# The first unit of a fused adaLN, linear attention and mixture-of-experts kernel: a new order for its zero products, norms, roundings and weight halves

## What the reference computes

```python
# x: (2, 2048, 256), 16 heads of 16, 8 experts of width 128, top 2
mod = (silu(c) @ wmod).reshape(2, 6, 1, 256)
sa, ca, ga, sb, cb, gb = (mod[:, k] for k in range(6))
ga, gb = (sign(g) * maximum(abs(g), 0.25) for g in (ga, gb))
h = layernorm(x) * (1 + ca) + sa
Q, K, V = (h @ W.T + b for W, b in ((Wq, bq), (Wk, bk), (Wv, bv)))
Q, K = elu(Q) + 1, elu(K) + 1
KV = einsum('bshd,bshe->bhde', K, V)
Z = 1 / (einsum('bshd,bhd->bsh', Q, K.sum(axis=1)) + 1e-6)
x = x + ga * (einsum('bshd,bhde,bsh->bshe', Q, KV, Z) @ Wo.T + bo)
h = layernorm(x) * (1 + cb) + sb
logits = (h / norm(h)) @ (centroids / norm(centroids)).T + h @ w_route.T
gates = softmax over the two largest logits
x = x + gb * sum_e gates_e * (gelu(h @ w1_e + b1_e) @ w2_e + b2_e)
```

## Time and profile before

| | us |
|---|---|
| median of three runs | 365.79 |
| the three runs | 365.43, 365.79, 366.67 |
| profiled execution | 366.65 |
| its span, first to last instruction | 364.6 |
| TensorE (PE) busy | 349.9 (96%) |
| VectorE (DVE) busy | 286.7 (79%) |
| GpSimd (POOL) busy | 260.5 (71%) |
| ScalarE (ACT) busy | 234.0 (64%) |

### The profile page before, as it was taken

How to read it: one execution, slowest core, us unless ns; L and a number is a source line. 1 busy time by engine, 2 the same in 40 slices (tenths; PEclk the granted TensorE clock), 3 DMA queues, 4 the chain that set the end, 5 groups by cost and what they waited for, 6 DMA issues and landing times.

```text
span 364.6 us, 8796 instructions
## 1 busy us (share of the span) xinstructions
PE 349.9 (96%) x2780; PEld 327.3 (90%) x2780; DVE 286.7 (79%) x820; ACT 234.0 (64%) x516; POOL 260.5 (71%) x358
## 2 busy tenths in 40 slices
PE   7999999998999996899999999999999999999995
PEld 7877888887888996899998999999999999999895
DVE  4769767567776989989999898898898988886754
ACT  4376787888978764648557485584674855855541
POOL 4346899877977667787897878889889877655210
PEclk9999999999999999999999999999999999999999
DMA  7941640000000032142240322422314314324211
GB/s 267 331 155 34 202 144 0 2 1 2 0 2 3 1 119 89 40 135 89 61 144 21 127 90 60 135 79 78 104 54 131 87 58 145 89 59 146 93 54 58
DMA packets 23713, 31.79 MB, mean 87 GB/s; under 512 B 2288, under 2 KB 14204, under 8 KB 23680
## 3 DMA queue, kind: packets, MB, share of 16 engines
q1 hardware_dynamic: 23240, 31.34, 27.6%
q10 hardware_dynamic: 440, 0.04, 0.1%
HBM read 27.04 MB, written 4.34 MB: 86 GB/s over the span
## 4 chain that ended last, share of the span: by engine, by line
PE 75%; DVE 16%; issue 4%; DMA 2%; ACT 2%; DVEq 0%; ACTq 0%
PE bank L795 21%; PE bank L796 19%; PE bank L797 19%; PE bank L803 4%; PE bank L850 3%; DVE hid_g L1348 2%; PE bank L827 2%; DMA g_bc<-in_b 2%; DVE bank L1365 2%; PE bank L978 2%; DVE early L1265 1%; PE bank L903 1%; DVE gT_f L1404 1%; PE bank L1020 1%; DVE den L1296 1%
## 5 line engine op out<-in xcount | busy, mean ns | idle before, releaser
L738 ACT ACTIVATE bank<-bank,cols_sb 128x256 f32<-128x256 f32 x128 | 51.3, 438 | 43.1 <-PE bank L797 42.8
L795 PE MATMUL bank<-tr_hi,w_hi 128*128 128x256 f32 x256 | 73.4, 287 | 0.0
L796 PE MATMUL bank<-tr_lo,w_hi 128*128 128x256 f32 x256 | 72.3, 282 | 0.0
L797 PE MATMUL bank<-tr_hi,w_lo 128*128 128x256 f32 x256 | 72.1, 282 | 0.0
L795 PE MATMUL bank<-w_hi,hid_pair 128*128 128x256 f32 x252 | 70.6, 280 | 0.0
L797 PE MATMUL bank<-w_hi,hid_pair 128*128 128x256 f32 x252 | 70.4, 279 | 0.0
L796 PE MATMUL bank<-w_lo,hid_pair 128*128 128x256 f32 x252 | 70.4, 279 | 0.0
L501 POOL TENSOR_TENSOR hid_pair<-hid_g,hid_pair 128x512 fp32r<-128x512 f32 x42 | 54.3, 1294 | 7.0 <-POOL gT_r L526 3.3
L795 PEld LDWEIGHTS bank<-tr_hi,w_hi 128*128 128x128 f32 x256 | 48.8, 191 | 0.3 <-DVE hid_g L1348 0.2
L797 PEld LDWEIGHTS bank<-tr_hi,w_lo 128*128 128x128 f32 x256 | 48.9, 191 | 0.0
L796 PEld LDWEIGHTS bank<-tr_lo,w_hi 128*128 128x128 f32 x256 | 48.8, 191 | 0.0
(11 more groups left out here) (161 smaller groups left out, 934.0 us busy)
## 6 DMA issues: line engine op xcount, KB each, us to landing
g_bc<-g_dram SPq DMA_DIRECT2D x64, 256.0 KB, 3.5
x_sb<-in_x SPq DMA_DIRECT2D x16, 256.0 KB, 3.7
out<-x_sb SPq DMA_DIRECT2D x15, 256.0 KB, 2.3
early<-in_wmod SPq DMA_DIRECT2D x3, 512.0 KB, 7.4
q_sb<-in_w SPq DMA_DIRECT2D x2, 512.0 KB, 6.4
q_sb<-in_w SPq DMA_DIRECT2D x1, 1024.0 KB, 10.3
mod_row<-mod_dram SPq DMA_DIRECT2D x1, 1024.0 KB, 6.6
q_sb<-in_wqkvT SPq DMA_DIRECT2D x2, 384.0 KB, 5.7
```

The costliest lines, as they stand in the source:

```text
L738: last = ac.activation(half, half, ACT.Gelu, bias=b1_sb[:, e:e + 1])
L795: te.matmul(out_ap, l_hi, r_hi, start=start, stop=False, skip_group_check=shared)
L796: te.matmul(out_ap, l_hi, r_lo, start=False, stop=False, skip_group_check=shared)
L797: return te.matmul(out_ap, l_lo, r_hi, start=False, stop=stop, skip_group_check=shared)
```

## The change

TensorE's first group of zero products grows from 14 to 24 and waits for b2_r's memset alone (zero_first), which VectorE now does first. The centroids' sum of squares moves on TensorE behind unit 0 and mod_rows(0); the clipping on VectorE behind bias_o; the power on GpSimd behind step_a of unit 1; split_route on VectorE behind step_a of unit 1. ScalarE rounds unit 0's activations. The low half of each chunk of wqkv is made right behind its rounding, the biases' low row ahead of unit 1's statistics, and the centroids' squares behind them.

```diff
-WARM = (14, 20)
+WARM = (24, 20)
@@ gpsimd
-            normalise_centroids()
             step_a(u0)
             step_a(unit(1))
+            normalise_centroids()
             step_a(unit(2))
@@ scalar
             modulate(u0, 0)
+            act.wait_ge(a_hf, 1)
+            ac.activation(tr_hi[:, 0, :, :], tr_f[:, 0, :, :], ACT.Copy).then_inc(a_hi, 1)
@@ tensor
-            pe.wait_ge(zero_rows, 1)
+            pe.wait_ge(zero_first, 1)
             for _ in range(WARM[0]):
                 te.matmul(bank[3][:, 0:E], b2_r[:, 0:P], b2_r[:, :], start=True, stop=True)
...
             tp_a(u0)
-            pe.wait_ge(cent_sq_ready, 1)
-            pe.wait_ge(modcol_ready, 1)
-            for c in range(NC):
-                last = te.matmul(bank[0][:, 0:NE], ones_f, cent_sq[:, c, :], start=(c == 0), stop=(c == NC - 1))
-            last.then_inc(cent_done, 1)
             for _ in range(WARM[1]):
...
-            pe.wait_ge(qkv_ready, 1)
+            pe.wait_ge(qkv_ready, NC)
             step_a(u0)
             mod_rows(0)
+            pe.wait_ge(cent_sq_ready, 1)
+            pe.wait_ge(modcol_ready, 1)
+            for c in range(NC):
+                last = te.matmul(bank[0][:, 0:NE], ones_f, cent_sq[:, c, :], start=(c == 0), stop=(c == NC - 1))
+            last.then_inc(cent_done, 1)
             step_a(unit(1))
@@ vector
-            for rows in (bqk_r[:, :], b2_r[:, :], gT_r[:, :, :], g_nat[:, :, :]):
+            ve.memset(b2_r[:, :].bitcast(F32), 0.0).then_inc(zero_first, 1)
+            for rows in (bqk_r[:, :], gT_r[:, :, :], g_nat[:, :, :]):
...
+            def low_weights(c):
+                dve.wait_ge(qkv_step, c + 1)
+                TT(wqkv_lo[:, c, :], wqkv_raw[:, c, :], wqkv_hi[:, c, :].bitcast(F32), ALU.subtract)\
+                  .then_inc(qkv_ready, 1)
...
             ve.tensor_copy(wqkv_hi[:, 0, :], wqkv_raw[:, 0, :]).then_inc(qkv_step, 1)
+            low_weights(0)
...
             ve.tensor_copy(wqkv_hi[:, 1, :], wqkv_raw[:, 1, :]).then_inc(qkv_step, 1)
+            low_weights(1)
+            dve.wait_ge(a_hi, 1)
+            TT(tr_lo[:, 0, :, :], tr_f[:, 0, :, :], tr_hi[:, 0, :, :].bitcast(F32), ALU.subtract).then_inc(a_lo, 1)
+            dve.wait_ge(bqk_step, 2)
+            TT(bqk_r[32:33, :], bqk_raw[32:33, :], bqk_t[32:33, :].bitcast(F32), ALU.subtract).then_inc(bqk_ready, 1)
+            stats_a(u0.plus(1))
             dve.wait_ge(d_small, 16 * N_SMALL)
             TT(cent_sq[:, :, :], route_raw[:, :, 0:NE], route_raw[:, :, 0:NE], ALU.mult).then_inc(cent_sq_ready, 1)
-            for c in range(NC):
-                dve.wait_ge(qkv_step, c + 1)
-                last = TT(wqkv_lo[:, c, :], wqkv_raw[:, c, :], wqkv_hi[:, c, :].bitcast(F32), ALU.subtract)
-            last.then_inc(qkv_ready, 1)
-            split_a(u0)
...
-            clip_centroids()
             stats_a(unit(2))
             split_b2()
-            split_route()
             step_a(u0)
             mod_rows(0)
             bias_o()
+            clip_centroids()
             step_a(unit(1))
+            split_route()
             mod_rows(1)
```

More of the change, by code:

```diff
@@ L206, in adaln_block @@
         qkv_step = sem("qkv_step"); qkv_ready = sem("qkv_ready")
-        zero_rows = sem("zero_rows"); warm_done = sem("warm_done"); ones_ready = sem("ones_ready")
+        zero_rows = sem("zero_rows"); zero_first = sem("zero_first"); warm_done = sem("warm_done"); ones_ready = sem("ones_ready")
         cent_done = sem("cent_done"); cent_n2_ready = sem("cent_n2_ready"); cent_ready = sem("cent_ready")
```

## The result

| | before | after |
|---|---|---|
| median of six runs each, on one chip (us) | 365.78 | 362.96 |
| lowest to highest | 365.33 to 366.67 | 362.53 to 363.94 |
| ratio, with its 95% interval | | 0.9922 (0.9909 to 0.9936) |
| profiled execution / its span | 366.65 / 364.6 | 362.67 / 360.9 |

The change is worth 0.8%, 2.8 us. The ratio and its interval are taken over all the runs, not from the two medians. The forecast of 364.8 had the direction, but was 1.8 us too high, and the time lies 0.44 us under the whole range.

The account below looks back on a forecast made before the run. TensorE, busy 349.9 of 364.6 us, was taken as the bound. A lead of 3.1 us at unit 1, less 1.25 us given back on VectorE, left 1.8: 366.65 - 1.8 = 364.85, said as 364.8; range 363.4 to 366.9 us.

Parts of the forecast that it names:

- Steps 1 to 5: Start-up to unit 1: clock up by 6.7 us, unit 0 at 11.6 instead of 16.22, unit 1 3.1 us earlier.
- third rival: TensorE's start: the clock does not rise in the first dense stretch, giving 367.5 us; chance 0.18.
- Step 6: VectorE's queue up to unit 3: 1.25 us given back, unit 3 at 35.25 instead of 37.05, lead 1.8 us.
- Term (a): VectorE's first split of expert weights: the last load lands at 20.9 us, so 0.7 us are lost.
- Term (c): VectorE ahead of splitting the route: waits 0.6 us for GpSimd's power of the norms, done at 30.05 us.
- (b): VectorE's busy stretch: the clipping of the norms now stands in it and adds 0.17 us.
- first rival: VectorE's stretch up to unit 3: its lateness does not reach TensorE, unit 1's lead stays, 363.6 us; chance 0.18.
- second rival: VectorE's backlog is larger: it waits the whole power, 1.3 us more, or the load lands 1 us later; 366.0 us, chance 0.14.

Follow-up runs that it names:

- after_again: The kernel after, unchanged, run again in another group: 363.19 us, ratio 0.9919.
- after_third: The kernel after, unchanged, run in a further group: 363.30 us, ratio 0.9923.
- late_landing: The kernel after, with the last load of expert weights queued behind Wo and unit 4's tokens: 364.40 us, ratio 0.9962.
- pad_vector: The kernel after, with two unused memsets (0.96 us) on VectorE ahead of its work for unit 1: 364.43 us, ratio 0.9963.
- before_again: One more traced execution of the kernel before, unchanged: 366.47 us, span 363.6 us, no interval.
- zeros_alone: The kernel before, with only b2_r's memset first and 24 early zero products instead of 14: 366.12 us, ratio 1.0012.
- norms_front_filled: The kernel after, norms' work put back in front, with 14 zero products between unit 0's transposes and the norms: 363.71 us, ratio 0.9927.
- norms_front: The kernel after, with all work of the centroids' norms put back where it stood before: 365.27 us, ratio 0.9988.
- warm14: The kernel after, with 14 first zero products instead of 24: 363.98 us, ratio 0.9953.
- stats_first: The kernel after, with unit 1's statistics ahead of the biases' low row on VectorE: 363.28 us, ratio 0.9927.

## Why the prediction was wrong in size

**Steps 1 to 5 held.** Predicted and found in the trace after: clock up ahead of the columns (1.8 us, 1.84), unit 0 at 11.6 (11.35), a stand of 1.3 us (1.03), transposes of unit 1 at 16.15 (15.83), unit 1 near 20.4 (20.25), its lead 3.1 (23.49 - 20.25 = 3.24). In after_again and after_third unit 0 comes at 11.83 and 11.81, the transposes at 16.32 and 16.30, so the forecast lies among the three. The third rival, a clock that doesn't rise, was not seen in a trace of this kernel.

**Step 6 failed.** It said that 1.25 us of that lead are given back before unit 3. None is: unit 3's lead is 37.05 - 33.78 = 3.27 us between the first traces, as large as unit 1's. The same can be read within each trace, where an execution's late start drops out. From unit 1's transposes to unit 3 the prediction had 35.25 - 16.15 = 19.1 us; the three traces of after have 17.95 or 17.96. That is 0.56 to 0.59 more than before, about the norms' products.

Two terms were mis-sized. Term (a), 0.7 us for the landing: predicted at 20.9 us, found at 19.6, and VectorE does not wait. It measured 0 in all three traces of the kernel after. Term (c), 0.6 us for the wait for the power: it measured 0.16 at most, 0.08 from the end of one instruction to the start of the next. The power ended at 28.65 us instead of 30.05. Of these 1.4 us, 0.7 are term (a) that did not cut GpSimd's lead, 0.3 that unit 1's transposes came earlier than forecast (15.83, not 16.15), 0.1 the clipping, and 0.3 that power and key sum were shorter than in the earlier trace rows (1.72 and 1.28 us instead of 1.89 and 1.40).

VectorE could lose about 1.0 us unseen: the slack of 0.55, and 0.5 by which its lead of 3.78 us at the second feature map of unit 0 (23.02 - 19.24) exceeded TensorE's. Steps (a), (b) and (c) took 2.1 from it. It lost 1.0: its lead at unit 3's rounding is 34.70 - 31.93 = 2.77 us. The parts are 0.08 for the clipping (23.88 to 23.96), 0.35 for a wait for ScalarE that nobody forecast, 0.69 at power and route (0.53 of it the route's three operations), less 0.15 by which the split of weights beside the key sum took less time than before. So the slack goes from 0.55 to 0.05, and nothing of it reached unit 3. late_landing and pad_vector show that the mechanism is there, one microsecond away: an extra 1 us reaches TensorE whole.

The first rival is what happened: "the power or the landing comes a little earlier and the stretch's waits close up". I gave it 0.18, since I read the landing off a single row. Its number, 363.6 us, was too high as well, by 0.6, for the reason in the next paragraph. The second rival worked out what a longer landing costs; what a shorter one gives back, by itself, I did not. In the third rival's sum I left out its own lead of 0.15 us: 1.4 - 0.55 - 0.15 = 0.7, so 367.35 us and not 367.5.

**The base.** The other half of the miss is no step of the change. I took the profiled execution's 366.65 and added nothing for its being 0.87 above the median. 365.78 - 1.8 would have been 364.0; the missing 1.0 us of gain makes the rest (2.8 instead of 1.8). Of the 3.98 us between the two first traces, 3.27 are there at unit 3, 0.4 come later in the span and 0.3 outside it. That the median gain is 2.82 and not 3.98 is scatter: 0.87 us for the one trace and 0.29 for the other. In after_again and after_third unit 3 starts at 34.28 and 34.25 us, 1.8 earlier than in before_again. That is the forecast's lead, and it is luck: step 6 took 1.25 us off, and these two executions started half a microsecond later than the first trace of after, before_again 1 us earlier than that of before.

**What I did not see.** The sum held without it, but the prediction priced moving the norms at what it issues (0.44 us against 1.02 + 0.50). In truth it is what puts dense products where the clock needs them: without it the 24 products gain nothing (zeros_alone), and with fill in its place they gain again (norms_front_filled). Until the squares are there nothing dense runs, and the 20 zero products behind them run at the low level, whether the clock fell in that wait (norms_front, near 9.9 us) or ahead of it (zeros_alone, near 8.0). The first trace could not show this: before the change the clock was low there anyway.

## What to carry to other kernels

A clock that has been raised must be kept to the first real work: a small step that depends on a late load, and makes TensorE wait 1.6 us as in norms_front, belongs behind the real work, or gets fill (products without use) in front of it. A duration of a transfer that lies on the path is worth a second trace before one builds a sum on it, and so is a start time that is compared between two traces; the base of a forecast is the median, not the execution that happened to be profiled. When a lead is won at the start, look at the slack of the engine that feeds the bound one: here 0.55 us became 0.05, and every further microsecond there counts in full.

## What the runs showed of the hardware that I had not expected

- The clock falls back sooner than I thought. After 24 dense products had raised it, 16 two-column instructions, 4 transposes and 1.64 us of idle time brought it to 0.50 by 10.5 us (norms_front), and in warm14 it fell within the stretch from 7.30 to 8.20 us, in the transposes, with no idle time behind the sparse instructions (1.23 us ahead of them). In stats_first it fell near 7.6 us behind 24 dense products, with 0.18 us of idle time. In all three traces of the kernel after, with the same instructions in the same order, it stayed up. So one program can do either; what decides it is not shown.
- 14 products of zeros (3.32 us), begun at 1.25 us, were followed by columns at the high level in warm14, where 3.36 us, begun at 2.41, were not the earlier trace rows. This execution of 14 did what the prediction thought only a longer stretch could. Across the traces with 24, their length is 4.44 to 5.49 us, so the clock rises at different points of the stretch.
- VectorE and GpSimd hold each other up. In the kernel after VectorE's split of weights beside GpSimd's key sum takes 1.09 us instead of 0.28, and goes on just when the key sum (to 26.97) is over:

```profile
26.04 1.09 DVE L1255 CAST w_hi<-q_sb 128x256 fp32r<-128x256 f32 x1
...
25.69 1.28 POOL L420 TENSOR_TENSOR hid_g<-hid_g,k_sb 128x512 f32<-128x512 f32 x1
```

  In the kernel before the low half of the same split stands beside the key sum of the earlier trace rows and takes 1.37 us instead of 0.43, so the loss only changes its place:

```profile
29.70 1.37 DVE L1250 TENSOR_TENSOR w_lo<-q_sb,w_hi 128x256 fp32r<-128x256 f32 x1
```

  The Trainium skill ("SBUF — State Buffer", section "Who interferes with whom") says that the two engines share a pair of ports as a lock, and that the later one stands still until the other's instruction is done; it names VectorE's copies and casts in a two-port mode, and its instructions with two inputs in SBUF beside a GpSimd instruction that reads SBUF. The traces agree, with 0.8 us for the cast and 0.9 for the subtraction; which mode the cast is in they don't show. The prediction left it out.
- The page's granted clock is 1.00 in the first microseconds, although the products' distances (0.22 us for 128x256) show the low level; after a fall it reads 0.50.
- A power on 128x8 takes GpSimd 1.64 to 1.90 us (norms_front, zeros_alone), wherever it stands, where the subtraction on 64 times the elements (128x512) takes 1.30.
